# Splitting the latents of the second cross-attention: one root, masked keys inside the loop, four buffers

## What is computed

```python
def _layernorm(x, axis=-1, eps=1e-05):
    return (x - mean) / sqrt(var + eps)

# second cross-attention: latents = _layernorm(x), rows = ctx_1024
xn = layer_norm(rows, g_x, b_x)
ln = layer_norm(latents, g_l, b_l)          # a second root over the first one's result
q  = ln @ Wq
kv = concatenate([xn, ln], axis=1) @ Wkv
sim = where(mask, q @ k.T, max_neg)         # some context keys are masked
out = softmax(sim) @ v
```

## Time and profile before

| what | value |
| --- | --- |
| median of 3 runs | 1310.88 us (1310.04 to 1312.64) |
| profiled execution | 1310.83 us, its span 1308.7 us |
| busy share of the span: PE, DVE, ACT, POOL | 79%, 67%, 67%, 67% |
| the stage split1, from DVE's first to PE's next work | 424.67 to 471.54 us |

### The profile page before, as it was taken

The page is one execution under the profiler, slowest core; times in us unless marked ns, Lnnn a source line. Parts: engine busy times, 40 slices in busy tenths (PEclk is TensorE's granted clock), DMA queues, the critical chain, the costliest instruction groups (busy, mean ns, idle before and its releaser), DMA issues.

```text
span 1308.7 us, 36650 instructions
## 1 busy us (share of the span) xinstructions
PE 1035.4 (79%) x13473; PEld 815.3 (62%) x13473; DVE 878.0 (67%) x2479; ACT 876.3 (67%) x1830; POOL 879.7 (67%) x994
## 2 busy tenths in 40 slices
PE   0569899994887459999999999999999981288860
PEld 0445677772544248888887878788787860266640
DVE  5789788885886966666675667767666741266645
ACT  0559899982664548888887878878887861166540
POOL 1170799993676737768778788788878886357661
PEclk9859555556998579999999999999999985599995
DMA  9995000000222001111211322131212211222216
GB/s 219 255 284 123 8 16 15 17 17 5 38 44 49 1 1 30 31 34 27 50 33 39 47 37 57 32 62 34 51 39 39 55 34 50 79 67 78 81 35 193
DMA packets 188834, 78.67 MB, mean 60 GB/s; under 512 B 118463, under 2 KB 184938, under 8 KB 188667
## 3 DMA queue, kind: packets, MB, share of 16 engines
q1 hardware_dynamic: 168859, 62.23, 22.1%
q0 software_dynamic: 4544, 8.67, 2.2%
q10 hardware_dynamic: 15264, 5.51, 1.7%
HBM read 19.54 MB, written 30.47 MB: 38 GB/s over the span
## 4 chain that ended last, share of the span: by engine, by line
PE 46%; POOL 7%; issue 4%; DVE 3%; another core or an unknown queue 2%; DMA 1%; ACT 1%; SPq 1%; POOLq 0%; ACTq 0%; DVEq 0%
PE bank L1399 11%; PE bank L1445 6%; PE bank L1893 4%; PE bank L1431 4%; PE bank L1427 4%; PE bank L1428 4%; PE bank L1429 4%; PE bank L1469 3%; PE bank L1416 3%; PE bank L1905 2%; POOL tokens L1317 2%; DVE X L1988 1%; POOL attention_pl_l L1223 1%; POOL attention_pl_c L1223 1%
## 5 line engine op out<-in xcount | busy, mean ns | idle before, releaser
L1661 DVE TENSOR_REDUCE attention_negmax<-bank 128x2 f16<-128x410 f32 x256 | 137.8, 580 | 152.6 <-PE bank L1416 152.1
L1223 POOL TENSOR_TENSOR attention_pl_l<-attention_probs_l,attention_ph_l 128x512 f16<-128x512 f32 x128 | 148.4, 1159 | 89.6 <-ACT attention_ph_l L1544 86.9
L636 POOL TENSOR_TENSOR attention_probs_l<-attention_probs,attention_probs_h 77x512 f16<-77x512 f32 x128 | 145.3, 1152 | 52.8 <-ACT attention_probs_h L718 48.6
L1223 POOL TENSOR_TENSOR attention_pl_c<-attention_probs_c,attention_ph_c 77x512 f16<-77x512 f32 x128 | 147.7, 1154 | 0.0
L2010 POOL DMA_INDIRECT outputs<-layer_kv x78 | 86.7, 1112 | 65.5 <-ACT layer_kv L1946 35.5
L1431 PEld LDWEIGHTS bank<-identh,attention_negmax 128*128 128x128 f16 (+1 forms) x1024 | 83.7, 107 | 56.3 <-issue 1.0
L1399 PE MATMUL bank<-layer_kv,ah 128*128 128x128 f16 x1024 | 108.4, 220 | 11.9 <-PEq L2123 11.8
L1445 PE MATMUL bank<-attention_vh_l,attention_ph_l 128*128 128x65 f16 x512 | 95.8, 195 | 17.9 <-POOL attention_pl_c L1223 17.9
L1399 PE MATMUL bank<-v1h,layer_kv 128*128 128x256 f16 (+1 forms) x512 | 105.8, 274 | 1.5 <-DVE attention_vl_c L1668 1.5
L1655 DVE SCALAR_TENSOR_TENSOR attention_tl<-bank,attention_th 128x512 f16<-128x512 f32 x128 | 87.8, 686 | 24.3 <-ACT attention_th L1535 24.3
L1544 ACT ACTIVATE attention_probs_l<-bank 128x512 f32<-128x512 f32 x128 | 76.2, 596 | 37.0 <-PE bank L1431 35.6
(11 more groups left out here) (370 smaller groups left out, 4089.0 us busy)
## 6 DMA issues: line engine op xcount, KB each, us to landing
tokens<-blank SPq DMA_DIRECT2D x1, 18360.0 KB, 71.0
layer_kv<-tokens SPq DMA_DIRECT2D x39, 136.0 KB
ctx<-outputs SPq DMA_DIRECT2D x8, 512.0 KB, 5.7
X<-in_x SPq DMA_DIRECT2D x4, 512.0 KB, 9.3
attention_pay<-attention_pay SPq DMA_DIRECT2D x8, 256.0 KB
out<-X ACTq DMA_DIRECT2D x8, 256.0 KB, 4.6
attention_turned_h<-attention_heads_h SPq DMA_TRANSPOSE x96, 2.2
attention_turned_l<-attention_heads_l SPq DMA_TRANSPOSE x96, 2.4
```

The source lines that it names most:

```text
L636: pool.tensor_tensor(probs_l[:, n % SLOTS], probs[:, n % 2], probs_h[:, n % SLOTS], ALU.subtract).then_inc(p_split, 1)
L1223: last = pool.tensor_tensor(low[:, g % 2], whole[:, g % 2], high[:, g % 2], ALU.subtract)
L1661: last = dve.tensor_reduce(negmax[:, g, 2 * i:2 * i + 2], score[i], AX.X, ALU.max, negate=True)
```

## The change

- `latent_scale` has one root. The product of the two roots is 1 / sqrt(v) with v = var * (1 + eps) + eps * eps (the `rsqrt` adds eps itself), so one tensor_scalar makes v from var and one `rsqrt` of twelve instructions follows. The first root and the three products go.
- Job x has depth 4: four `normed` and `whole` buffers and four PSUM banks (banks 2 to 5), and the semaphores are opened by 4. Its chunks are written out, no longer looped. Job ctx keeps depth 2, and so do both jobs of the first layer's split, the one called `split0`.
- `mask_keys` is no longer behind the loop but in it: DVE normalises chunk k, then makes plane 2 of chunk k - 2, for ten steps. Each chunk takes four instructions on 4 sequences (subtract, copy, multiply, add) with two waits on its own results, one between subtract and multiply with the copy between, one between multiply and add. It waits for that chunk's copies by ACT in both jobs.

```diff
-    def __init__(self, name, rows, src, hi, lo, by=None, mean=None, rstd=None, shift=None, gain=None, bias=None):
+    def __init__(self, name, rows, src, hi, lo, by=None, mean=None, rstd=None, shift=None, gain=None, bias=None, depth=2, behind=None):
...
-            job.banks = [bank[2 * at + u][:, 0:CH * rows].rearrange("p (c r) -> p c r", r=rows) for u in range(2)]
+            job.banks = [bank[2 * at + u][:, 0:CH * rows].rearrange("p (c r) -> p c r", r=rows) for u in range(job.depth)]
...
-            if job.by == "vector":
+            if job.by == "vector" and job.depth == 2:
...
-                    body(k, k % 2)
+                    body(k, k % job.depth)
...
-                if job.by == "vector":
+                if job.by == "vector" and job.behind is None:
                     chunks(dve, job, lambda k, u: normalise(dve, job, k, u))
+                elif job.by == "vector":
+                    behind = job.behind(m)
+                    for k in range(NCH + 2):
+                        if k < NCH:
+                            normalise(dve, job, k, k % job.depth)
+                        if k >= 2:
+                            behind(dve, k - 2)
...
-                pe.sem_inc(job.turned, 2)
+                pe.sem_inc(job.turned, job.depth)
...
-                    act.wait_ge(job.turned, k + 3)
+                    act.wait_ge(job.turned, k + job.depth + 1)
...
-        diff = m.sb("diff", [D, 2, B // 2, C], FP16)
-        steps = m.sem("steps")
...
-            for job in jobs:
-                dve.wait_ge(job.high, NCH + 2)
...
+        diff = m.sb("diff", [D, 2, CH, C], FP16)
...
+            x, part = slice(CH * k, CH * k + CH), diff[:, k % 2]
+            first = kv[:, x, 0, 0:1].broadcast_to([D, CH, C])
+            dve.wait_ge(ctx_job.high, k + 1 + ctx_job.depth)
+            dve.wait_ge(x_job.high, k + 1 + x_job.depth)
+            dve.tensor_tensor(part, kv[:, x, 0, S:KV], first, ALU.subtract).then_inc(told_apart, 1)
+            dve.tensor_copy(kv[:, x, 2, 0:S], kv[:, x, 0, 0:S])
+            dve.wait_ge(told_apart, k + 1)
+            dve.tensor_tensor(part, part, w.mask01[:, x, :], ALU.mult).then_inc(masked, 1)
+            dve.wait_ge(masked, k + 1)
+            dve.tensor_tensor(kv[:, x, 2, S:KV], part, first, ALU.add)
...
             row_statistics(dve, link, w, bn)
-            rsqrt(dve, link, r[:], w.mv[:, :, 1], t1[:], t2[:])
-            link(dve.tensor_tensor(v[:], r[:], r[:], ALU.mult))
-            link(dve.tensor_tensor(v[:], v[:], w.mv[:, :, 1], ALU.mult))
+            link(dve.tensor_scalar(v[:], w.mv[:, :, 1], 1.0 + EPS, EPS * EPS - EPS, ALU.mult, ALU.add))
             rsqrt(dve, link, w.rstd[:], v[:], t1[:], t2[:])
-            link(dve.tensor_tensor(w.rstd[:], w.rstd[:], r[:], ALU.mult))
...
-                              "vector", w.mv, w.rstd, gain=gain_l, bias=bias_l)]
-                split_transposed(nc, w, bank, "split1", jobs, before=latent_scale(w), after=mask_keys(w, kv, jobs))
+                              "vector", w.mv, w.rstd, gain=gain_l, bias=bias_l, depth=4)]
+                jobs[1].behind = mask_keys(w, kv, jobs)
+                split_transposed(nc, w, bank, "split1", jobs, before=latent_scale(w))
```

More of the change, by code:

```diff
@@ L397 @@
 class Split:
-    def __init__(self, name, rows, src, hi, lo, by=None, mean=None, rstd=None, shift=None, gain=None, bias=None):
+    def __init__(self, name, rows, src, hi, lo, by=None, mean=None, rstd=None, shift=None, gain=None, bias=None, depth=2, behind=None):
         self.name, self.rows, self.src, self.hi, self.lo = name, rows, src, hi, lo
         self.by, self.mean, self.rstd, self.shift, self.gain, self.bias = by, mean, rstd, shift, gain, bias
+        self.depth, self.behind = depth, behind
 def split_transposed(nc, w, bank, tag, jobs, before=None, after=None):
@@ L412, in split_transposed @@
             n, rows = job.name, job.rows
-            job.normed = m.sb(f"normed_{n}", [rows, 2, CH, D]) if job.by else None
-            job.whole = m.sb(f"whole_{n}", [128, 2, CH, rows])
+            job.normed = m.sb(f"normed_{n}", [rows, job.depth, CH, D]) if job.by else None
+            job.whole = m.sb(f"whole_{n}", [128, job.depth, CH, rows])
             job.ready, job.turned, job.high, job.split = (m.sem(f"{x}_{n}") for x in ("ready", "turned", "high", "split"))
-            job.banks = [bank[2 * at + u][:, 0:CH * rows].rearrange("p (c r) -> p c r", r=rows) for u in range(2)]
+            job.banks = [bank[2 * at + u][:, 0:CH * rows].rearrange("p (c r) -> p c r", r=rows) for u in range(job.depth)]
         chain = m.sem("chain")
@@ L480, in copy @@
                     last.then_inc(job.high, 1)
-                act.sem_inc(job.high, 2)
+                act.sem_inc(job.high, job.depth)
                 chunks(act, job, copy)
@@ L489, in low @@
                     chunk = bass.ds(k * CH, CH)
-                    pool.wait_ge(job.high, k + 3)
+                    pool.wait_ge(job.high, k + job.depth + 1)
                     pool.tensor_tensor(job.lo(chunk), job.whole[:, u], job.hi(chunk), ALU.subtract).then_inc(job.split, 1)
@@ L493, in low @@
                         normalise(pool, job, k + 2, u)
-                pool.sem_inc(job.split, 2)
+                pool.sem_inc(job.split, job.depth)
                 if job.by == "gpsimd":
@@ L1075, in memory, with work @@
     def memory(m):
-        diff = m.sb("diff", [D, 2, B // 2, C], FP16)
-        steps = m.sem("steps")
-        def work(dve, link):
-            for job in jobs:
-                dve.wait_ge(job.high, NCH + 2)
[L1082 to L1093, removed]
+        diff = m.sb("diff", [D, 2, CH, C], FP16)
+        told_apart, masked = m.sem("told_apart"), m.sem("masked")
+        ctx_job, x_job = jobs
+        def work(dve, k):
+            x, part = slice(CH * k, CH * k + CH), diff[:, k % 2]
[8 more added lines that the diff above has]
+            dve.tensor_tensor(kv[:, x, 2, S:KV], part, first, ALU.add)
         return work
@@ L1100, in memory @@
     def memory(m):
-        t1, t2, r, v = (m.sb(n, [S, B]) for n in ("t1", "t2", "r", "v"))
+        t1, t2, v = (m.sb(n, [S, B]) for n in ("t1", "t2", "v"))
         bn = m.sb("bn", [S, B, 6])
```

## The result

The changed kernel is slower: 1323.18 us (median of 4 runs, 1322.79 to 1323.69) against 1311.76 us (4 runs, 1310.04 to 1314.24) for the kernel before beside it, a ratio of 1.0078, interval 1.0048 to 1.0109. The forecast was 1310.8 us with a range to 1313.4. The profiled span went from 1308.7 to 1321.1 us.

The account below looks back on a forecast made before the run. DVE was taken to bound the stage from job x's start, itself set by POOL through PE, to its end. Terms of -0.1, -3.7, +2.3 and +1.3 us gave about -0.2 to 0: 1310.8 us, range 1308.2 to 1313.4.

Parts of the forecast that it names:

- Start of job x set by POOL through PE, roots worth nothing: Job x's start follows POOL's ctx job through PE, so dropping a root gains only 0.1 us: 443.8 for 443.92.
- the upper bound given (0.3): Largest gain allowed at job x's start, with the loop's register instructions on DVE gone too: 0.3 us.
- Pieces: Masked keys on DVE cut into eight pieces of 1.31 us, 10.5 us against 8.15 before: cost 2.3 us.
- POOL's locks: All eight POOL subtracts of job x hold up a busy DVE, 0.88 us each, together 7.0 us: cost 1.3 us.
- Idle time gone: In job x, 3.7 of DVE's 3.98 us of idling come back; 0.3 us stays before the first masked piece.
- End of the stage: DVE's last instruction ends at 470.4 us against 470.41 before; the first matmul of `second_half` starts at 471.5.
- the sum: Start -0.1, idle -3.7, pieces +2.3, locks +1.3, rest rounding: about -0.2 to 0 us, so 1310.83 us becomes 1310.8.

Follow-up runs that it names:

- root_only: The kernel before with only the two roots replaced by one, loop and masked keys as they were: 1308.76 us, ratio 0.9996.
- pool_unrolled: The kernel before with job x's chunks written out on POOL alone, the other engines keeping the loop: ratio 1.0063, experts' stage 146.2 us.
- after_looped: The changed kernel with job x's chunks in a loop again on PE, ACT and POOL: 1308.92 us, ratio 0.9997 to the kernel before.
- pe_unrolled: The kernel before with job x's chunks written out on PE alone, the other engines keeping the loop: ratio 0.9995.
- before_pad60_b: The kernel before with 60 idle increments on POOL ahead of its first send of the experts' stage, on the first chip: ratio 0.9992.
- after_pad12_b: The changed kernel with 12 idle increments on POOL ahead of its first experts' send, on the first chip: 1312.83 us, ratio 1.0012 to the kernel before.
- after_again: The changed kernel repeated unaltered on the first chip, as a control: 1320.92 us, ratio 1.0068 to the kernel before.
- after_third: The changed kernel unaltered, on a fourth chip: 1302.10 us, ratio 0.9991 to the kernel before.
- after: The changed kernel as first measured and profiled: 1323.18 us, ratio 1.0078 to the kernel before.

## Why the prediction was wrong

By its own steps:
- *Start of job x set by POOL through PE, roots worth nothing*: right. Released by PE's line 473 after 5.67 us of idling, at 443.37 for 443.8 forecast. The stage's first statistics were 0.26 us earlier (424.41 for 424.67), and 0.29 us is the gain beyond that, near the upper bound given (0.3), not the 0.1 chosen. `root_only` confirms that the roots are worth nothing.
- *Pieces*: right. A piece without disturbance has a pitch of 1.33 us (452.44 to 453.77), forecast 1.31. From multiply to add are 0.34 us, where 0.22 + 0.13 were forecast. The Trainium skill, VectorE: DVE Perf Modes, section "The DRAIN you can't avoid", would have had 0.22, by the same rate: the pitch speaks against it here.
- *POOL's locks*: right in kind and number. Eight DVE instructions are drawn out for job x, six by 0.81 us and two by 0.96, together 6.8 us where 7.0 were forecast. The ctx job's last two subtracts cost 0.82 us more (the first twelve steps take 3.97 us, 3.16 without), where the prediction counted one, at 0.44; the earlier start hides it.
- *Idle time gone*: right. 0.15 us are left before the first piece, where 0.3 were forecast, and 0.09 before the last.
- *End of the stage*: DVE ends at 470.33, forecast 470.4; first matmul at 471.48, forecast 471.5. On chips that don't tip, and with the loop kept, the whole is 0.9991 and 0.9997 of before, as forecast.

The step that failed is the one behind the sum: "The profiled execution of 1310.83 us [...] becomes 1310.8". It took over everything after the stage unchanged, on the ground that its start was unchanged. The change also writes out a loop on PE, ACT and POOL, and of this the prediction priced only the register instructions that go, on DVE. That such an edit moves the rest of POOL's program against its fetches was no term, no bound and no rival, and the range held nothing from outside the stage. The trace of before had the signs: the late part of the experts' stage runs at another pace from 1240 us on, with the same ACT wait of 4.5 us, so that this stage could be tipped, and what a tip at its start would cost could be worked out: (3.76 - 3.27) us a tile for the 24 tiles between sends 4 and 52 is 11.8 us, with the slow pace of the changed kernel; measured 9.8. In place of "unchanged", the runs showed this stage 9.8 us longer (145.4 for 135.7), brought on by POOL's written-out loop alone (`pool_unrolled`, 146.2 us).

Shown: of the change's parts, POOL's written-out loop is enough (`pool_unrolled`), and without it the others cost nothing (`after_looped`, `root_only`, `pe_unrolled`); twelve idle instructions take the stall at send 4 away; a single delay of POOL tips the stage until its end; whether it tips depends on the chip, and the chips that tip are those on which PE's increments come late. Argued only: that the fetch at send 0 is the trigger. It is there in all six profiles and absent in twelve, but it makes no send late, and in `before_pad60_b` no stall follows the fetch at send 23, while the stall at send 52 stays though the fetch of send 47 has moved away. Open: how POOL's program reaches PE's increments, why PE pauses, why the slow pace keeps itself up, what tips the kernel before at send 52 and the profiled run of `after_pad12_b` at 12, and why the chips differ.

## What to carry to other kernels

A sum for one stage is a forecast for the kernel only if the later stages are indifferent to when, and by what program, they are reached: look in the trace of before for a stage that runs at two paces, and put the difference into the range as a rival. Writing out a loop moves every later instruction in its engine's program; keep the loop, or test the same edit alone, before the gain or loss is given to the part that was meant. A record that starts late is not yet a delay: look whether it also ends late, and whether the next one does. Measure on more than one chip when a result rests on a stage of hand-overs between four engines.

## What the runs showed of the hardware that was not expected

- The changed kernel is 0.7% slower than the one before on one chip (`after_again`) and level with it on another (`after_third`, 0.9991 [0.9982, 1.0001]); the kernel before itself takes 1308.6 to 1311.8 us on some chips and 1303.0 to 1303.4 us on others. It shows in one stage: 136 us in the kernel before, 127 us in its padded and delayed variants on a quick chip.
- On the chips with the slow pace, PE's semaphore increments come late, at nearly the same places of the program in every profile (by up to 0.84 us ahead of the experts' stage, by over 3 us in its stalls); on the two others none comes over 0.09 us behind the modelled end of the matmul. In `after` the three due at 1158.45, 1159.72 and 1159.94 come at 1160.56, 1160.68 and 1160.74.
- Program arrives by DMA in transfers of 8192 bytes, which for POOL fit 128 instructions. One that falls on the first indirect DMA after a long wait goes with a record that starts 0.3 us later and is 0.3 us shorter; the next send starts no later.
- One delay of 1.8 us on an engine with a third of its time to spare cost 10 us, because the pipeline didn't return to its pace.
- An indirect DMA of POOL that waits for a memset of POOL's own starts 0.77 us after its end, against 0.30 us between two sends without such a wait.
